# ScalarE does hidT before swish in each step of the experts stage

## The reference

```python
t = _rmsnorm(x, norm_scale)
g = t @ gate_w.T + gate_b
vals, idx = jax.lax.top_k(gf, K)                 # 4 of 32 experts for each of 4096 tokens
w = jax.nn.softmax(vals, axis=-1)
h1 = jnp.einsum('th,efh->tef', tf, w1) + b1
h = _swiglu(h1)                                  # glu * sigmoid(1.702 * glu) * (lin + 1), clipped at 7
out = jnp.einsum('tef,ehf->th', h * combine, w2) + combine @ b2

x = x + 0.5 * ffn(layernorm(x))
x = x + attention(layernorm(x))
x = x + 0.5 * ffn(layernorm(x))
```

## Time and profile before

| | us |
|---|---|
| median of 3 executions | 726.49 (726.35 to 728.78) |
| the profiled execution, its own time | 724.5 |
| its span in the trace | 722.8 |
| experts, first layer | about 112 to 289 |
| experts, second layer | about 459 to 633 |

### The profile page before, as it was taken

How to read it: one execution, slowest core, us unless ns; L and a number is a source line. 1 busy time by engine, 2 the same in 40 slices (tenths; PEclk the granted TensorE clock), 3 DMA queues, 4 the chain that set the end, 5 groups by cost and what they waited for, 6 DMA issues and landing times.

```text
span 722.8 us, 12887 instructions
## 1 busy us (share of the span) xinstructions
PE 525.7 (73%) x3232; PEld 443.3 (61%) x3235; DVE 437.0 (60%) x1243; ACT 347.9 (48%) x752; POOL 505.3 (70%) x551
## 2 busy tenths in 40 slices
PE   6258887999999998395607864999999999834000
PEld 3154266999898997163504552699989999734000
DVE  7889223555457778388993877255555767744222
ACT  4444414666566665495607743366656666511000
POOL 3677777777437777777677777777752777777765
PEclk9557999999999999697558955999999999967555
DMA  7997115666556664221111111466655666424222
GB/s 267 390 382 287 54 52 166 199 198 197 177 164 196 199 197 154 64 55 53 48 51 55 51 52 54 137 199 208 203 183 161 197 199 204 153 72 126 65 63 57
DMA packets 56491, 108.26 MB, mean 150 GB/s; under 512 B 12576, under 2 KB 19968, under 8 KB 56320
## 3 DMA queue, kind: packets, MB, share of 16 engines
q1 hardware_dynamic: 40064, 74.13, 30.9%
q0 software_dynamic: 16384, 33.59, 16.1%
HBM read 51.00 MB, written 56.62 MB: 149 GB/s over the span
## 4 chain that ended last, share of the span: by engine, by line
PE 48%; POOL 17%; DVE 13%; issue 11%; ACT 6%; DMA 4%; POOLq 0%; DVEq 0%; ACTq 0%; SPq 0%
PE PS L1242 19%; PE PS L1137 11%; PE PS L1255 10%; POOL xs L535 10%; POOL YG L560 6%; ACT swish L668 3%; PE PS L1356 2%; DMA xrow<-xs 2%; DVE PS L986 1%; DMA xs<-U,row 1%; DMA YG<-ys,row 1%; PE PS L1342 1%; DVE st L717 1%; PE PS L1317 1%; DVE chosen L777 1%
## 5 line engine op out<-in xcount | busy, mean ns | idle before, releaser
L560 POOL DMA_INDIRECT YG<-ys,row x256 | 245.5, 959 | 117.7 <-issue 77.5
L535 POOL DMA_INDIRECT xs<-U,row x256 | 249.4, 974 | 81.9 <-issue 73.2
L1242 PE MATMUL PS<-W,xT 128*128 x768 | 183.1, 381 | 0.2 <-DVE glulin L931 0.2
L1242 PEld LDWEIGHTS PS<-W,xT 128*128 128x128 f32 x768 | 139.0, 191 | 16.1 <-issue 0.9
L931 DVE TENSOR_SCALAR glulin<-PS 128x512 f32<-128x512 f32 x96 | 66.4, 691 | 127.8 <-PE PS L1255 100.0
L625 ACT ACTIVATE yrow<-PS 128x512 f32<-128x512 f32 x96 | 57.3, 597 | 108.7 <-PE PS L1255 108.7
L1255 PEld LDWEIGHTS PS<-W,hidT 128*128 128x128 f32 x768 | 99.9, 191 | 14.4 <-issue 10.0
L1255 PE MATMUL PS<-W,hidT 128*128 x768 | 102.3, 276 | 7.0 <-ACT hidT L633 6.9
L944 DVE SCALAR_TENSOR_TENSOR hid<-glulin,swish 128x512 f32<-128x512 f32 x96 | 66.7, 694 | 15.9 <-ACT swish L629 15.2
L637 ACT ACTIVATE xT<-PS 128x512 f32<-128x512 f32 x96 | 56.5, 589 | 38.8 <-PE PS L1137 38.8
L629 ACT ACTIVATE swish<-glulin 128x512 f32<-128x512 f32 x96 | 60.5, 630 | 22.3 <-DVE glulin L931 14.1
(11 more groups left out here) (178 smaller groups left out, 710.3 us busy)
## 6 DMA issues: line engine op xcount, KB each, us to landing
xrow<-xs SPq DMA_DIRECT2D x96, 256.0 KB
ys<-yrow SPq DMA_DIRECT2D x96, 256.0 KB, 2.2
xs<-YG SPq DMA_DIRECT2D x6, 2048.0 KB, 13.4
W<-in_w12T SPq DMA_DIRECT2D x1, 6144.0 KB
xs<-U,row POOLq DMA_INDIRECT x256
YG<-ys,row POOLq DMA_INDIRECT x256
out<-X SPq DMA_DIRECT2D x7, 256.0 KB, 2.5
X<-in_x SPq DMA_DIRECT2D x4, 256.0 KB, 3.7
```

Of the source, the lines that this page charges most:

```text
L535: pool.indirect_dma_start(out=xs[c], out_offset=bass.IndirectOffsetOnAxis(ap=row[:, i:i + 1], axis=0), in_=U[:, (c * CT + t) * H:(c * CT + ...
L560: pool.indirect_dma_start(out=YG[:, t * TOPK + k, :], out_offset=None, in_=ys[c], in_offset=bass.IndirectOffsetOnAxis(ap=row[:, i:i + 1], ...
L1242: last = te.matmul(h1, xT[:, s, q * P:(q + 1) * P], W[:, bass.ds(es[q], 2 * H)], start=True, stop=True)
```

## The change

In each step of the experts stage ScalarE makes hidT (group k-3) before swish (group k-2). The waits move with their instructions; the other engines' programs and ScalarE's yrow and xT are unchanged.

```diff
                     if live(k, 4, NGF):
...
                         a.activation(yrow[:, r, :], YP, ACT.Copy).then_inc(yrow_ready, 1)
+                    if live(k, 3, NGF):
+                        act.wait_ge(turned, k + (t0 + 1))
+                        wait_count(act, multiplied, k + (m0 - 2 + apart))
+                        a.activation(hidT[:, s, :], HT, ACT.Copy).then_inc(hidT_ready, 1)
                     if live(k, 2, NGF):
                         act.wait_ge(glu_ready, k + (g0 - 1))
                         wait_count(act, hid_ready, k + (g0 - 3))
                         a.activation(swish[:, r, :], glu[:, r, :], ACT.Gelu_apprx_sigmoid).then_inc(swish_ready, 1)
-                    if live(k, 3, NGF):
-                        act.wait_ge(turned, k + (t0 + 1))
-                        wait_count(act, multiplied, k + (m0 - 2 + apart))
-                        a.activation(hidT[:, s, :], HT, ACT.Copy).then_inc(hidT_ready, 1)
                     if live(k, 0, NGF):
```

## The result

The changed kernel took 731.44 us (median of 9), the kernel before 726.49 (median of 9): ratio of the fast runs 1.0045, 95% interval 1.0027 to 1.0064. That is 3.3 us slower by the ratio (the medians lie 4.95 us apart), inside half a per cent but outside the range of the forecast (724.7 to 728.6), and on the side that was given 0.10 as rival C.

What follows compares the result with a forecast made beforehand. TensorE was taken to bound steady experts, GpSimd's DMAs the pass ends. First pass -0.3 and second +0.4 us gave +0.1: 724.6 us profiled, 726.6 median after carrying over 2.0; range 724.7 to 728.6.

Steps and rivals of the forecast that it cites:

- rival C: Experts passes: moved hids collide with GpSimd DMAs every three steps, 0.38 us each; +2.8 us, 729.3 to 730.5; chance 0.10.
- the steady step: Experts, mid-pass: hidT 0.86, swish 1.35, xT 1.88, hid 2.10 us after yrow; step stays 3.49 us, cost 0.
- The wait of 0.72 us at 219.09: First experts pass: TensorE's wait for hidT behind a late swish was to go, its gain hidden by the gather.
- the last groups: End of each experts pass: hidT 0.49 us sooner, then hid late; last yrow moves by -0.3 us, bounds -0.6 and 0.
- GpSimd is never held by its counters: Experts passes: GpSimd's waits on ScalarE's and TensorE's counters do not hold its DMAs, always 0.30 us idle between.
- One sign: Sign of a wrong forecast: TensorE waiting for hid or glulin inside the passes, or a step longer than 3.49 us.
- GpSimd's term: DMAs lengthened by moved hids: first scatter +0.3, first gather -0.6, second scatter +0.6, second gather +0.6 us against 0.77 cover.
- The rule: GpSimd DMA starts: 1.26 us apart (1.25 in gathers), plus 0.56 us less the distance when just behind a hid.
- with the hids moved by 0.62: GpSimd's DMA layout: every old hid start shifted 0.62 us later, 0.35 in steps where VectorE also adds gathered rows.
- the bounds: Extra DMA time: first scatter +0.2 to +0.4, first gather -0.6 to +0.8, second scatter -0.6 to +0.7, second gather +0.6 to +1.7.
- The milder lock also exists for moved hids: Argument against rival C: the collision of 0.1 to 0.25 us every four steps can also hold after the change.
- There VectorE waits for the gather: End of first experts pass: VectorE waits for the gather, so TensorE's gains, the 0.72 us included, are hidden: 0.

Runs made afterwards that it cites:

- e6: The kernel before with hidT ahead of swish only in the last steps of each experts pass; one pair only, 727.27 us beside 723.19 for before.
- e1d: The kernel before with only VectorE's hid made later, by also waiting for hidT, ScalarE's order untouched; ratio to before 1.0066, median 730.58 us.
- e2d: The changed kernel with lin clipped in place in PSUM, so hid reads one SBUF input; ratio to before 0.9963, median 722.57 us.
- e3d: The kernel before with lin clipped in place in PSUM, so hid reads one SBUF input; ratio to before 0.9976, median 723.54 us.
- e4d: The kernel before with hidT ahead of swish in the first experts pass only; ratio to before 1.0018 (0.9998 to 1.0039), median 727.52 us.
- late runs: Runs of 853 to 889 us with every kernel, before included, engines starting late for unknown reasons; the changed kernel's ratio to before there 0.9956.

## Why the prediction was wrong

Right, by its own steps: every start in the steady step shown within 0.01 us, the step of 3.49 us, the granted clock of 1.00 in it. The wait of 0.72 us at 219.09 is gone. In the last groups the wait fell from 1.34 to 0.83 us (forecast 0.8), the next transposes then waited for hid as foreseen, and the last yrow came 0.35 us sooner relative to its pass (forecast 0.3; e6 shows the same). GpSimd is never held by its counters. One sign did turn up, small: hid is transposed 3.64 us behind T, 0.85 behind the end of the moved hid, and beside additions that is used up. The loads of these transposes start 0.05 and 0.06 us behind hid's end at 220.86 and 567.59 of the changed kernel, and the two steps take 3.79 and 3.67 us instead of 3.49. That the price, if any, lies where hid meets GpSimd was the argument too; e1d, e2d and e3d show that this is the cause.

Wrong: the size of GpSimd's term. The rule was good. Laid on the hids of the changed kernel's own trace it gives the last starts of the two scatters as 191.92 and 538.73 (they are 191.93 and 538.74) and of the gathers as 292.29 and 638.71 (292.37 and 638.80). The failed step is "with the hids moved by 0.62": I moved the old starts all by one amount. They were not evenly spaced, and the pattern of collisions lives on that. In the second scatter hid had come 1.46 to 1.65 us behind yrow; in the changed kernel it comes 2.02 to 2.12 behind. Before:

```profile
505.21 0.95 POOL L535 DMA_INDIRECT xs<-U,row  x1 [0.30 <-issue]
505.22 0.71 DVE L944 SCALAR_TENSOR_TENSOR hid<-glulin,swish 128x512 f32<-128x512 f32 x1 [0.19 <-ACT swish L629]
...
508.51 0.69 DVE L944 SCALAR_TENSOR_TENSOR hid<-glulin,swish 128x512 f32<-128x512 f32 x1 [0.19 <-ACT swish L629]
508.99 1.04 POOL L535 DMA_INDIRECT xs<-U,row  x1 [0.30 <-issue]
```

One hid 3.29 us behind the last, and the DMA falls 0.48 behind it, where a collision costs 0.08 us: the mild pattern, once in four steps. In the changed kernel hid hangs on the transposes instead of on glulin, and its spacing there is 3.41 to 3.58:

```profile
504.21 0.69 DVE L944 SCALAR_TENSOR_TENSOR hid<-glulin,swish 128x512 f32<-128x512 f32 x1 [0.73 <-ACT swish L633]
504.40 1.33 POOL L535 DMA_INDIRECT xs<-U,row  x1 [0.30 <-issue]
...
514.77 0.69 DVE L944 SCALAR_TENSOR_TENSOR hid<-glulin,swish 128x512 f32<-128x512 f32 x1 [0.90 <-ACT swish L633]
514.88 1.41 POOL L535 DMA_INDIRECT xs<-U,row  x1 [0.30 <-issue]
```

Three steps and eight DMAs apart, 0.37 and 0.45 us each: the lock that rival C described, in all four stretches. Three of them came out beyond even the bounds (0.2 to 0.4, -0.6 to 0.8, -0.6 to 0.7 forecast against 0.6, 1.5 and 1.5 measured; the second gather, 1.6, within 0.6 to 1.7).

The scatters of the other traces bear the spacing out. Where, a few steps into the pass, it is 3.40 to 3.59 us (the first scatter with either order, in before, e4d and e6 too, and the second of the changed kernel and e1d), the extra is 2.4 to 3.1 us; where it runs from 3.28 to 3.61 (the second scatter with the old order: before, e4d, e6) it is 0.85 to 1.15. So the first scatter had little to lose: the old order alone gives 2.45 in one execution and 2.8 in another. Laid on yrow's starts of before plus the 2.10 us that I had worked out, the same rule gives 2.5 us for the second scatter, near the 2.7 measured; for the gathers it gives only 1.5 and 1.7 against 3.5 and 3.1, so a tenth or two in the starts still decide there. How little the forecast of 1.8 could bear shows in its first hid: leave that one unmoved and the rule gives 7 long ones and 1.8 us, move it with the rest and it gives 4 and 0.5.

C's price, +2.8 us, is close to the 3.3 measured, in part by luck: it has 1.2 us for the first pass and 1.6 for the second, where the joints show 0.9 and 2.3. Its chance of 0.10 was too low. "The milder lock also exists for moved hids" rested on moving unevenly spaced starts.

The end of the first pass was wrong too. "There VectorE waits for the gather" took VectorE as what goes on; it is GpSimd's next gather, with 1.19 us of idle time as cover, as in the second pass. So what counts there is the last yrow. By the forecast's own terms it moves by +0.3 (scatter), -0.3 (last groups) and -0.7 (the wait at 219.09): -0.7 us for the first pass instead of -0.3, further from what was measured. With the extras as measured it is this cover that kept the first pass to 0.9 us.

The sum also lacked a term. A later scatter was passed on one to one; in e1d, e4d and e6 the granted clock falls behind the wait for xrow, for another 1.9 to 2.8 us from the last scatter to the gather. The changed kernel's profiled execution was free of it and took 728.4 us, near the fastest of its nine (728.18 to 732.98). Whether the slower ones had such a fall wasn't seen, since only one execution is profiled and their mean granted clocks (0.839 at 731.66 us, 0.832 at 728.18) are too coarse to tell.

The Trainium skill ("SBUF — State Buffer", Who interferes with whom) names the cause in the form that these runs bear out: two SBUF inputs on VectorE contend with a GpSimd instruction that reads SBUF. e2d and e3d agree: one input moved to PSUM, and no scatter DMA beside experts is longer than 0.97 us. The same page's figure for a block ("A bandwidth-pool intuition that's wrong": VectorE's end plus about 115 ns, measured there beside a tensor_copy) is again not what the rows show: the DMA of 504.40 ends 0.83 us behind hid's end, that is 0.96 us counted from 0.13 us before it.

## What to carry to other kernels

An engine with time to spare may still set the pace of another, as VectorE's hid does with GpSimd's DMAs here: when an instruction is moved, look at what it is moved onto, not only at who waits for it. Where two periodic streams collide, don't shift the old starts by a constant; ask which pattern is stable under even spacing, and give that one the greater chance. Best take the collision away: with one operand read from PSUM no cost of hid's place can be told, and in either order the kernel is faster than before (0.9963 and 0.9976).

## What the hardware showed that I had not expected

A wait of TensorE of about 1 us for data, with a further 0.86 us for hidT behind it, was followed by half speed in e4d (0.96 us) and e6 (1.26) but not in the changed kernel (1.02 and 1.05); 2.31 us in e1d was. A VectorE instruction that starts just behind an indirect DMA's start isn't delayed: the hid of 505.22, 0.01 us behind the DMA of 505.21, took 0.71 us instead of 0.69. And in the late runs the same change of order was worth 0.4% in the other direction: it trades slack on the path to TensorE against the place of hid.
